# A search for a threshold with two small operations a step, evenly spaced, in a fused feed-forward kernel

## What is computed

```python
def _L0_attn_ref(x, w_gate, w_up, w_down):
    s = jax.nn.silu(jnp.einsum('bsh,ih->bsi', x, w_gate))      # I = 2752
    k = int(0.5 * I)
    _, idx = jax.lax.top_k(-jnp.abs(s), k)                     # the k smallest magnitudes of a token
    flat = flat.at[rows, idx.reshape(B * S, k)].set(0.0)
    s = flat.reshape(B, S, I) * jnp.einsum('bsh,ih->bsi', x, w_up)
    return jnp.einsum('bsi,hi->bsh', s, w_down)

def _L0_ffn_ref(hidden_states, ...):
    routing_weights, _ = jax.lax.top_k(hidden_states @ gate_w, 2)
    h = jax.nn.relu(hidden_states @ up_w) ** 2
    shared_out = h @ down_w
    moe_out = (hidden_states @ fc1_w @ expert_w) * sum(routing_weights)
    return _layernorm(shared_out + moe_out @ fc2_w, ln_gamma, ln_beta)

xn = _layernorm(x)                                              # 2048 tokens x 1024
x = x + _L0_attn_ref(xn, ...) + _L0_ffn_ref(xn, ...)
```

## Time and profile before

| | |
|---|---|
| median of 3 runs | 2412.04 us (2411.74 to 2412.51) |
| profiled execution | 2412.13 us, span 2410.3 us |
| PE busy | 2373.4 us (98%), 10720 matmuls |
| DVE busy | 1519.5 us (63%) |
| ACT, POOL busy | 968.2 us (40%), 584.3 us (24%) |
| DMA, mean | 529.04 MB, 219 GB/s |
| mean granted TensorE clock | 0.996 |

### The profile page before, as it was taken

How to read it: one execution, slowest core, us unless ns; L and a number is a source line. 1 busy time by engine, 2 the same in 40 slices (tenths; PEclk the granted TensorE clock), 3 DMA queues, 4 the chain that set the end, 5 groups by cost and what they waited for, 6 DMA issues and landing times.

```text
span 2410.3 us, 27343 instructions
## 1 busy us (share of the span) xinstructions
PE 2373.4 (98%) x10720; PEld 1971.8 (82%) x10720; DVE 1519.5 (63%) x1757; ACT 968.2 (40%) x1049; POOL 584.3 (24%) x502
## 2 busy tenths in 40 slices
PE   8999999989999999999999999999999999999999
PEld 7888777877878888888888888888888888888887
DVE  3139999886201998888321399889731169988850
ACT  3347665322211787531110287651200148665010
POOL 5566868687200000004000010103100001010500
PEclk9999999999999999999999999999999999999999
DMA  7886868957765656665666666666566566566555
GB/s 274 327 290 232 311 230 320 305 184 288 252 235 187 198 192 193 193 211 178 220 230 195 191 195 195 193 210 193 194 227 208 188 197 193 194 195 213 184 187 179
DMA packets 168578, 529.04 MB, mean 219 GB/s; under 512 B 18176, under 2 KB 27392, under 8 KB 168448
## 3 DMA queue, kind: packets, MB, share of 16 engines
q1 hardware_dynamic: 168448, 527.28, 65.5%
HBM read 406.55 MB, written 120.65 MB: 219 GB/s over the span
## 4 chain that ended last, share of the span: by engine, by line
PE 88%; DVE 7%; POOL 2%; issue 2%; DVEq 1%; DMA 1%; ACT 0%; SPq 0%; POOLq 0%
PE bank L586 29%; PE bank L588 29%; PE bank L587 28%; DVE junk_v L813 2%; PE bank L606 1%; DVE prod L875 1%; POOL w L447 1%; DVEq L700 1%; DVE junk_v L821 1%; PE bank L597 1%; POOL w L443 0%; DVE prod L788 0%; DVE cand L808 0%; POOL squares L452 0%; DVE acc L893 0%
## 5 line engine op out<-in xcount | busy, mean ns | idle before, releaser
L813 DVE TENSOR_SCALAR_CACHE_REDUCE junk_v<-mag,cand 128x2816 bf16<-128x2816 f32 x248 | 780.3, 3146 | 9.0 <-DVE cand L808 0.2
L486 ACT ACTIVATE junk_s<-mag,cand 128x2816 uint8<-128x2816 f32 x248 | 655.6, 2643 | 323.8 <-DVE cand L808 314.7
L586 PE MATMUL bank<-w,tok 128*128 128x512 f32 (+1 forms) x1408 | 545.4, 387 | 8.3 <-DMA w<-split_w 3.6
L588 PE MATMUL bank<-w,tok 128*128 128x512 f32 (+1 forms) x1408 | 543.6, 386 | 0.0
L587 PE MATMUL bank<-w,tok 128*128 128x512 f32 (+1 forms) x1408 | 543.1, 386 | 0.0
L452 POOL TENSOR_TENSOR squares<-squares 128x512 f32<-128x512 f32 x64 | 67.5, 1057 | 1192.8 <-ACT hidden L531 1192.8
L447 POOL TENSOR_TENSOR w<-raw,w 128x512 fp32r<-128x512 f32 (+1 forms) x212 | 291.6, 1381 | 121.7 <-ACT w L474 112.1
L586 PEld LDWEIGHTS bank<-w,tok 128*128 128x128 f32 x1408 | 265.5, 189 | 60.9 <-DMA w<-split_w 5.3
L739 DVE TENSOR_SCALAR positive<-mag 128x2048 uint8<-128x2048 f32 (+2 forms) x28 | 27.6, 984 | 454.0 <-ACT mag L507 397.8
L588 PEld LDWEIGHTS bank<-w,tok 128*128 128x128 f32 x1408 | 265.1, 188 | 50.5
L587 PEld LDWEIGHTS bank<-w,tok 128*128 128x128 f32 x1408 | 265.5, 189 | 49.9
(11 more groups left out here) (91 smaller groups left out, 2638.5 us busy)
## 6 DMA issues: line engine op xcount, KB each, us to landing
w<-split_w SPq DMA_DIRECT2D x612, 512.0 KB, 4.1
split_w<-w SPq DMA_DIRECT2D x204, 512.0 KB, 5.3
rows<-x_dram SPq DMA_DIRECT2D x32, 512.0 KB, 4.8
raw<-w_down_dram SPq DMA_DIRECT2D x44, 256.0 KB, 4.7
raw<-w_gate_dram SPq DMA_DIRECT2D x40, 256.0 KB, 4.9
raw<-w_up_dram SPq DMA_DIRECT2D x40, 256.0 KB, 3.2
w<-split_w SPq DMA_DIRECT2D x24, 392.0 KB, 3.4
raw<-up_w_dram SPq DMA_DIRECT2D x32, 256.0 KB, 4.4
```

The costliest lines, as they stand in the source:

```text
L486: act.activation(junk_s[:, :, :], mag[:, :, t, :], ACT.Sign, scale=-1.0, bias=cand[:, t:t + 1], accum_out=cnt[:, t:t + 1]).then_inc(counte ...
L586: pe.matmul(out, left[0], right[0], start=first, stop=False)
L588: return pe.matmul(out, left[1], right[0], start=False, stop=last)
L813: dve.tensor_scalar(junk_v[:, :, :], mag[:, :, t, :], cand[:, t:t + 1], float(1 - (GATED - KEPT)), ALU.is_lt, ALU.add, accum_out=cnt[:, t: ...
```

## The change

The search carries `cand` from step to step and never forms `thr` until the end. A step is now two small operations: `refused` (L805 of the changed kernel) is the bit as an integer where the count was too high, and else 0; `cand` (L808) is the old `cand` with the next bit set by *or* and the refused bit taken back by *exclusive-or*. The last such operation writes `thr`. The steps stand three granule numbers apart throughout, so the search ends at 145 in place of 153, and the masks after it stand earlier. Two more parts come with it: POOL's square and DVE's subtraction of a hidden tile stand two granule numbers later (`SQUARE_LAG`), and SP's loop (`BEHIND`) issues a granule's load for block 1 together with the store five granule numbers on, so that it no longer stands ahead of the next stores.

```diff
-    SEARCH_AT[_last + 3 + (len(SEARCH_AT) % 2 if len(SEARCH_AT) >= BITS // 2 else 0)] = len(SEARCH_AT)
+    SEARCH_AT[_last + 3] = len(SEARCH_AT)
...
+SQUARE_LAG = 2
+BEHIND = RING - 1
...
-    return 1 + k * (3 + NV)
+    return 1 + k * (2 + NV)
...
-        step = sb("step", [P, TILES], F32)
+        refused = sb("refused", [P, TILES], I32)
...
-            for b in range(BLOCKS):
-                for m in range(GRANULES):
+            for g in range(BLOCKS * GRANULES + BEHIND):
+
+                if g < GRANULES:
+                    sp.wait_ge(lo_ready, g + 1)
+                    if g + RAW < GRANULES:
+                        load_raw(g + RAW)
+                    store_split(g)
+                if g >= BEHIND and g - BEHIND + RING in range(GRANULES, BLOCKS * GRANULES):
+                    b, m = divmod(g - BEHIND, GRANULES)
+                    granule_read(sp, granule_used, bank_filled, b, m)
                     if b == 0:
-                        sp.wait_ge(lo_ready, m + 1)
-                        if m + RAW < GRANULES:
-                            load_raw(m + RAW)
-                        store_split(m)
-                    if b * GRANULES + m + RING in range(GRANULES, BLOCKS * GRANULES):
-                        granule_read(sp, granule_used, bank_filled, b, m)
-                        if b == 0:
-                            sp.wait_ge(split_stored[m % RING], 16 * (m // RING + 1))
-                        load_split(b * GRANULES + m + RING)
+                        sp.wait_ge(split_stored[m % RING], 16 * (m // RING + 1))
+                    load_split(g - BEHIND + RING)
+                if g - BEHIND in range(GRANULES - 1, BLOCKS * GRANULES, GRANULES):
+                    for t in range(TILES):
+                        store((g - BEHIND) // GRANULES, 1, t)
+                if g not in range(GRANULES, GRANULES + BEHIND):
+                    b, m = divmod(g if g < GRANULES else g - BEHIND, GRANULES)
...
-                    if m in HIDDEN_AT:
-                        i, t = HIDDEN_AT[m]
+                    if m - SQUARE_LAG in HIDDEN_AT:
+                        i, t = HIDDEN_AT[m - SQUARE_LAG]
                         pool.wait_ge(operand_hi, highs(b, "hidden", i * TILES + t + 1))
...
-                act.wait_ge(search, b * SEARCHES + searched(k) + 1)
+                act.wait_ge(search, b * SEARCHES + searched(k))
...
-                at = b * SEARCHES + searched(k) + 1 + NV
+                at = b * SEARCHES + searched(k) + NV
+                bit = 1 << (BITS - 1 - k)
+                after = cand if k + 1 < BITS else thr
                 dve.wait_ge(counted, (b * BITS + k + 1) * NS)
                 dve.wait_ge(search, at)
-                dve.scalar_tensor_tensor(out=step[:, :], in0=cnt[:, :], scalar=float(PAD + 1), in1=cand[:, :],
-                                         op0=ALU.is_le, op1=ALU.mult).then_inc(search, 1)
+                dve.tensor_scalar(refused[:, :], cnt[:, :], float(PAD + 1), float(bit), ALU.is_gt,
+                                  ALU.mult).then_inc(search, 1)
                 dve.wait_ge(search, at + 1)
-                dve.tensor_tensor(thr[:, :], thr[:, :], step[:, :], ALU.max).then_inc(search, 1)
-                dve.wait_ge(search, at + 2)
+                dve.scalar_tensor_tensor(out=after[:, :].bitcast(I32), in0=cand[:, :].bitcast(I32), scalar=bit >> 1,
+                                         in1=refused[:, :], op0=ALU.bitwise_or, op1=ALU.bitwise_xor).then_inc(search, 1)
...
-                dve.wait_ge(search, at)
-                dve.tensor_scalar(cand[:, :].bitcast(I32), thr[:, :].bitcast(I32), 1 << (BITS - 1 - k), None,
-                                  ALU.bitwise_or).then_inc(search, 1)
...
-                    if m - 1 in HIDDEN_AT:
-
-                        i, t = HIDDEN_AT[m - 1]
+                    if m - SQUARE_LAG - 1 in HIDDEN_AT:
+
+                        i, t = HIDDEN_AT[m - SQUARE_LAG - 1]
...
-                        dve.memset(thr[:, :], 0.0).then_inc(search, 1)
+                        dve.memset(cand[:, :].bitcast(I32), 1 << (BITS - 1)).then_inc(search, 1)
```

More of the change, by code:

```diff
@@ L412, in _ @@
                             load_rows(b + 1, t)
-                for t in range(TILES):
-                    store(b, 1, t)
             sp.wait_ge(stored, 16 * (2 * TILES * BLOCKS + 1))
@@ L793, in settle @@
             def settle(b, k):
-                at = b * SEARCHES + searched(k) + 1 + NV
+                at = b * SEARCHES + searched(k) + NV
+                bit = 1 << (BITS - 1 - k)
+                after = cand if k + 1 < BITS else thr
                 dve.wait_ge(counted, (b * BITS + k + 1) * NS)
                 dve.wait_ge(search, at)
-                dve.scalar_tensor_tensor(out=step[:, :], in0=cnt[:, :], scalar=float(PAD + 1), in1=cand[:, :],
-                                         op0=ALU.is_le, op1=ALU.mult).then_inc(search, 1)
+                dve.tensor_scalar(refused[:, :], cnt[:, :], float(PAD + 1), float(bit), ALU.is_gt,
+                                  ALU.mult).then_inc(search, 1)
                 dve.wait_ge(search, at + 1)
-                dve.tensor_tensor(thr[:, :], thr[:, :], step[:, :], ALU.max).then_inc(search, 1)
-                dve.wait_ge(search, at + 2)
+                dve.scalar_tensor_tensor(out=after[:, :].bitcast(I32), in0=cand[:, :].bitcast(I32), scalar=bit >> 1,
+                                         in1=refused[:, :], op0=ALU.bitwise_or, op1=ALU.bitwise_xor).then_inc(search, 1)
             def search_bit(b, k):
                 at = b * SEARCHES + searched(k)
-                dve.wait_ge(search, at)
-                dve.tensor_scalar(cand[:, :].bitcast(I32), thr[:, :].bitcast(I32), 1 << (BITS - 1 - k), None,
-                                  ALU.bitwise_or).then_inc(search, 1)
                 for i, t in enumerate(VECTOR_TILES):
-                    dve.wait_ge(search, at + 1 + i)
+                    dve.wait_ge(search, at + i)
                     dve.tensor_scalar(junk_v[:, :, :], mag[:, :, t, :], cand[:, t:t + 1], float(1 - (GATED - KEPT)),
```

## The result

| | before | after |
|---|---|---|
| median, 4 runs each | 2411.89 us (2410.87 to 2412.51) | 2388.07 us (2387.33 to 2391.4) |
| ratio, 95% interval | | 0.9904 [0.9892, 0.9916] |
| profiled execution | 2412.13 us | 2391.4 us, span 2389.6 |
| PE busy | 2373.4 us (98%) | 2368.0 us (99%) |
| DVE busy, instructions | 1519.5 us, 1757 | 1466.2 us, 1633 |

The change takes 23.8 us off, 1.0% (interval 0.8% to 1.1%); 20.0 were forecast. The profiled execution of after began its first granule 3.4 us later than that of before (40.82 against 37.38 us), and the other three runs are 3.1 to 4.1 us shorter. The profiled executions differ by 20.7 us; with the 3.4 us of the later start this makes 24.2, and this is the sum that the trace has to account for.

The account below looks back on a forecast made before the run. PE was taken as the bound, 98% busy, lacking work only in and just after block 0, where DVE and POOL delay it. Gains of 3.2 + 10.7 + 6.1 = 20.0 us off 2412.13 gave 2392.0 us, range 2379 to 2403.

Parts of the forecast that it names:

- the three terms named: Gains forecast in block 0, granules 48 to 152 (3.2 us) and 152 to 168 (10.7), and between blocks (6.1).
- The turn of blocks: Block 0 to block 1: SP's stores issued ahead of loads bring back 27 missing matmuls, gaining the whole 6.1 us.
- The squares: Block 0: two granules' lag gives ACT 5.4 us more a tile, ending PE's 9.7 us wait on POOL's weight splits.
- The search and the chain on DVE: Block 0: two small operations take 33 us, the chain 287.3; PE waits 10.0 us, and 3.2 of 14.8 are gained.
- Granules 152 to 168: Block 0: PE's 7.1 us wait on DVE's read of up banks and its clock dip go, gaining 10.7 us.
- The turned products: Block 0: PE's 3.1 us wait, from DVE's norm work among POOL's products, is left alone; gain 0.
- The floor: Block 0: if two small operations cost under 0.74 us a step, DVE keeps up; 2380.5 us, chance 0.22.
- The waits move: Block 0: collisions with POOL move to the two remaining small operations, 17.6 us above the forecast's cost; 2409.7 us, chance 0.18.
- The slower rival: All blocks: the new integer forms cost more a step than taken, 2482 us at 1.0 us extra; chance 0.05.
- The cover: Blocks 1 to 3: reorder is free; up(0)'s read ends before granule 152, with 6.7 us spare in block 1.

Follow-up runs that it names:

- experiment 3: Kernel before, with only POOL's squares and DVE's subtractions of hidden tiles two granule numbers later: 2408.1 us, ratio 0.9985.
- experiment 1: Changed kernel with the square lag at 0 and SP's old loop, leaving the two-operation search with even spacing: 2398.8 us, ratio 0.9945.
- Experiment 6: Changed kernel with the read of up(0) moved from granule number 147 to 145, ahead of the search's end: 2381.79 us, ratio 0.9872.
- experiment 7: Changed kernel with the high parts of block 0's weights up to granule 143 made by ACT instead of POOL: 2410.69 us, ratio 0.9992.
- experiment 9: Kernel of Experiment 6 with two more POOL operations a granule in block 1, granules 52 to 167, on unused buffers: 2382.02 us, one run.
- experiment 2: Kernel before, with only SP's new loop of stores and loads: 2405.71 us, ratio 0.9971.

## Why the prediction was right, and where it was off

**Direction and kind** held: 23.8 us off against 20.0, by the three terms named, with blocks 1 to 3 unchanged. The terms fit less well than their sum: 3.2, 10.7 and 6.1 us were forecast, and the trace has 10.3 (granules 48 to 152), 7.7 (152 to 168) and 6.2. Two errors, +7.1 and -3.0, partly cancel; 1.6 of each is only that I counted the dip in the first stretch and it fell into the second.

**The turn of blocks:** 6.1 us taken, 6.19 measured in the trace and 6.0 with SP's order alone.

**The squares:** PE's waits on splits went, as forecast. The cause was only half right. The lag removes them (experiment 3), but so does the shorter step, nearly (experiment 1).

**The search and the chain on DVE** was the step that was off. It said that PE would wait 10.0 us in all, half of it at granule 127, and that a dip would cost 1.6. The read's first tile was done at 453.9, which is 281.7 us behind the first count, where the sum said 287.3. Counted so that no moment is counted twice, the chain was (forecast in brackets): counts and their tails 200.2 (200.0), the two small operations 27.4 (33.0), 25 tiles of reads 15.0 (15.6), subtractions 16.2 (16.3), `drop_ties` with its branch 18.8 (18.5), the mask 4.1 (2.7), and no wait on the squares (1.2 kept). The term that was too large is the two small operations, and in it the 5.1 us that I added to 27.9 for waits that come back. None came back: the first two operations of a step took 522 + 343 = 865 ns before, and the two of after take 486 + 376 = 862. (The 28.6 us above contain 1.2 us in which `refused` begins while the operation ahead of it ends.)

PE waited 4.2 us at granule 152. The last hidden tile, to which I gave half of the wait, cost 0.15: DVE had the tile done at 381.56, 4.8 us earlier on the same reckoning than I had it (382.9 + 3.45), and the next matmul began at 381.70. Against that the dip was sized too small: it lasted 6.8 us, not 3.4, and cost 3.0. Left over were 7.5 us of the 25.5 in granules 48 to 168; I had left 11.6. These 4.1 us are the whole difference between 20.0 and the trace's 24.2 but for 0.1 at the turn.

**Granules 152 to 168:** the 7.1 us wait on L788 is gone, as forecast; 10.7 us were to come back and 7.7 did, as the dip of granule 152 (3.0 us) lies in this stretch.

**The turned products:** 0 taken, 4.0 us before and after.

**The rivals.** The floor (2380.5) needed under 0.74 us a step; it was 0.92. Experiment 6 reached it (2381.8) by another way, the read's place. "The waits move" had its mechanism right: `refused` takes 486 ns in block 0 against 223 in block 1, and what it pays it pays to POOL. But in this kernel nothing moved, since `step` in the same place took 522 ns already. No row told me how the phases would fall, and that they fell as well as they did was luck: in experiment 7 `cand` takes 757 ns, and the two cost 30.9 us. The Trainium skill ("SBUF — State Buffer", section "SBUF: two separate sides") has DVE and GpSimd take their shared port pair as an exclusive lock for a whole instruction; experiments 7 and 9 agree with it in kind, with `cand` at 304.70 held until 305.84, just behind the end of the first of the two POOL operations that began at 304.53. The slower rival is out: in block 1 the integer forms take 223 and 163 ns in the mean, and the float ones took 191 and 192.

**The cover:** no wait of PE in blocks 1 to 3; the read of up(0) was done 8.0 us ahead of granule 152 in block 1, where the sum had 6.7 us spare.

## What to carry to other kernels

A small operation in a dependent chain costs what the engine beside it makes of it: 0.17 us alone, and here, beside POOL, 0.27 to 0.90 us in the mean by its place in the step and its phase. Count such operations in the stretch where the other engine works, price one from that stretch, and look at its phase too, since less work of the neighbour can cost more. Then ask of every read that frees a bank whether it needs to stand behind the chain: moving four tiles of 0.6 us ahead of it gave 6.3 us. And a wait that is removed in front of another engine's late chain gives less than its length: the lag took 9.7 us ahead of granule 152 and gave 3.6. The three parts of this change gave 12.9, 6.0 and 3.6 us alone, 22.5 in sum, and 23.8 together.

## What the runs showed that I had not expected

- The small operations' price goes by phase: with POOL's high parts taken away, 22.7 + 8.2 us busy against 11.3 + 15.1, because ACT's split ties POOL's operation to the end of the search step. In all five traces looked at, every small operation over 0.25 us ends within 30 ns of a POOL operation's end.
- The half-clock stretch behind a wait of PE came as 3.4, 6.8 or 10.2 us: three of the four in the kernel before had 3.4, the one behind the 4.2 us wait at granule 152 in after 6.8, and one in experiment 2 had 10.2. Half of the part in which PE works is lost: 3.0 us in after.
- POOL's splitting made DVE's small operations, 0.16 to 0.22 us in the mean in block 1, 1.8 to 5.3 times as long in block 0 of before and after. The subtractions of 0.84 us became 0.97 to 1.10, and the counts of 3.15 us did not change.
